# A recommendation tower whose table gathers are given places in the order of work, two by two

## What is computed

```python
e = jnp.stack([tbl_0[ids[:, 0]], ..., tbl_39[ids[:, 39]]], axis=1)        # 2048 x 40 x 32
z = jnp.einsum('bke,kef,bkf->bk', e[:, I], W, e[:, J])                     # 780 pairs i < j
h = jnp.concatenate([z, dense_ctx], axis=1)                                # 2048 x 796
h = jnp.maximum(h @ W_top1 + b_top1, 0.0)                                  # 512
h = jnp.maximum(h @ W_top2 + b_top2, 0.0)                                  # 256
y = h @ W_top3                                                             # 1
```

## Time and profile before

| | us |
|---|---|
| timed, median of 3 | 632.92 |
| profiled execution, span of its core | 1130.1 |
| TensorE (matmul) busy in it | 875.4 |
| VectorE busy | 540.3 |
| POOL busy | 412.3 |
| ScalarE busy | 327.1 |

### The profile page before, as it was taken

How to read it: one execution, slowest core, us unless ns; L and a number is a source line. 1 busy time by engine, 2 the same in 40 slices (tenths; PEclk the granted TensorE clock), 3 DMA queues, 4 the chain that set the end, 5 groups by cost and what they waited for, 6 DMA issues and landing times.

```text
span 1130.1 us, 16792 instructions
## 1 busy us (share of the span) xinstructions
PE 875.4 (77%) x7232; PEld 201.8 (18%) x7232; DVE 540.3 (48%) x510; ACT 327.1 (29%) x243; POOL 412.3 (36%) x436
## 2 busy tenths in 40 slices
PE   4322358788779995886895789779889787899998
PEld 1000012121112220121121112112112111122223
DVE  3100067364345660452380447337245264688884
ACT  4001047553246380032260134127244000000002
POOL 6777341533353137324517151451624604000000
PEclk8555598887578895886796788989779788899999
DMA  4100044201001020100101002010010102011010
GB/s 155 32 14 13 12 145 127 63 7 52 9 11 53 12 72 13 44 16 18 38 22 41 5 10 75 9 47 4 12 34 8 39 3 58 8 39 29 1 36 3
DMA packets 30489, 39.24 MB, mean 35 GB/s; under 512 B 11376, under 2 KB 19200, under 8 KB 30160
## 3 DMA queue, kind: packets, MB, share of 16 engines
q1 hardware_dynamic: 14880, 25.59, 7.7%
q0 software_dynamic: 13824, 7.11, 4.3%
q10 hardware_dynamic: 1712, 5.48, 1.4%
HBM read 21.93 MB, written 0.07 MB: 19 GB/s over the span
## 4 chain that ended last, share of the span: by engine, by line
PE 65%; another core or an unknown queue 17%; issue 11%; DVE 3%; ACT 2%; SPq 1%; DMA 1%; DVEq 0%; ACTq 0%
PE t_ps L857 27%; PE z_ps L881 18%; PE x_ps L898 10%; PE x_ps L806 7%; PE x_ps L911 2%; SPq L543 1%; DVE prod L727 1%; ACT one_hot L602 1%; PE t_ps L911 1%; DVE one_hot L689 1%; PE t_ps L898 1%; PE t_ps L829 0%; DVE z_sb L673 0%; ACT one_hot L605 0%
## 5 line engine op out<-in xcount | busy, mean ns | idle before, releaser
L727 DVE TENSOR_TENSOR prod<-t_ps,e_t 128x1024 f32<-128x1024 f32 x392 | 459.4, 1213 | 425.2 <-remote 300.6
L558 POOL DMA_INDIRECT rows<-cold_tables,idx x432 | 412.1, 954 | 550.1 <-DVE e_t L734 420.2
L857 PE MATMUL t_ps<-e_t,w_sb 32*64 32x512 f32 x3120 | 362.0, 658 | 73.8 <-issue 53.6
L881 PE MATMUL z_ps<-prod,select 128*32 128x512 f32 x1560 | 243.5, 639 | 21.7 <-issue 21.0
L602 ACT ACTIVATE one_hot<-hot_sb,row_number 128x2048 bf16<-128x2048 f16 (+1 forms) x75 | 140.6, 1875 | 110.3 <-remote 87.4
L898 PE MATMUL x_ps<-z_sb,w_sb 128*32 128x512 f32 x704 | 131.1, 635 | 24.4 <-issue 22.5
L605 ACT ACTIVATE one_hot<-one_hot 128x2048 bf16<-128x2048 bf16 (+1 forms) x75 | 134.3, 1791 | 2.4
L857 PEld LDWEIGHTS t_ps<-e_t,w_sb 32*64 32x64 f32 x3120 | 74.6, 136 | 323.0 <-issue 221.6
L806 PE MATMUL x_ps<-one_hot,tables 128*32 128x512 bf16 x1194 | 97.8, 402 | 27.3 <-issue 22.6
L806 PE MATMUL t_ps<-one_hot,tables 128*32 128x512 bf16 x198 | 45.3, 501 | 92.1 <-issue 87.9
L689 DVE TENSOR_SCALAR one_hot<-hot_sb,row_number 128x2048 bf16<-128x2048 f16 (+1 forms) x47 | 33.9, 744 | 133.2 <-remote 130.0
(11 more groups left out here) (33 smaller groups left out, 98.6 us busy)
## 6 DMA issues: line engine op xcount, KB each, us to landing
e_t<-e_t SPq DMA_DIRECT2D x64, 128.0 KB
e_t<-e_t SPq DMA_DIRECT2D x112, 64.0 KB
rows<-cold_tables,idx POOLq DMA_INDIRECT x432
hot_sb<-hot_ids SPq DMA_DIRECT2D x11, 512.0 KB, 3.6
w_sb<-w_lay ACTq DMA_DIRECT2D x1, 1792.0 KB, 7.0
z_sb<-hot_tables SPq DMA_DIRECT2D x4, 320.0 KB, 5.1
w_sb<-w_lay ACTq DMA_DIRECT2D x1, 1216.0 KB
w_sb<-w_lay ACTq DMA_DIRECT2D x1, 896.0 KB, 4.6
```

The costliest lines, as they stand in the source:

```text
L558: pool.indirect_dma_start(out=rows[:, slot, span, :], out_offset=None, in_=table, in_offset=bass.IndirectOffsetOnAxis(ap=idx[:, n, span:sp ...
L727: nc.vector.tensor_tensor(prod[:, u % PROD_SLOTS, 0:banks, :], t_ps[:, at:at + banks, :], by, ALU.mult).then_inc(mult_done, 1)
L857: mm = nc.tensor.matmul(t_ps[cols, at + n, :], w_sb[part, b, cols], e_t[part, e_slot(k, of[side]), :], start=True, stop=True)
L881: mm = nc.tensor.matmul(z_ps[E * q:E * q + E, :], select[:, E - PER - PER * s:2 * E - PER - PER * s], prod[:, (u + q // 2) % PROD_SLOTS, q ...
```

## The change

`ORDER` is replaced by another string of 837 letters with the same steps, three of whose one-hots are VectorE's instead of ScalarE's (50 `o`, 72 `O`). A list `PACE` gives each item a first place and, by the next entry, an end. The 16 gathers of an item are issued in twos (`TOGETHER = 2`), each two at a place of its own, spread evenly between the item's first place and its end. Before each two POOL waits until the last generating burst ahead of that place has been multiplied by VectorE, or the last lookup ahead of it has been done, whichever of the two kinds stands last in the order. The wait for the slot stays. The core of the diff:

```diff
 ORDER = """
-pippppipphpoohoOppoohopphpohOppohpoophphpopohhhooOhpoohpohhopohphhpotopOhhohhhpgpoophhhphOhrhoohhoooppghhhOooh
...
+pppppippopooppOppihohpohhphhoopoopoppOopphhoohoOhOpppohohhopphhhohohhOoohphhpgohpohOhprhohhpohohpoophhhooOhoOg
...
+PACE = [
+    0, 59, 89, 119, 149, 179, 209, 251, 275, 299, 330, 354, 382, 406, 445, 469, 493, 517, 541, 565,
+    589, 613, 637, 661, 685, 709, 733, 763,
+]
+TOGETHER = 2
+
+
+def pace_of(n, span):
+
+    begin, end = PACE[n], PACE[n + 1]
+    return begin + (end - begin) * (span - span % TOGETHER) // SPANS
...
+        def wait_for_pace(engine, place):
+
+            for kind, *of in reversed(steps[:place]):
+                if kind == "gen":
+                    engine.wait_ge(mult_done, first_unit(*of) + 2)
+                    return
+                if kind == "hot" and of[2] < blocks[of[1]] - 1:
+                    engine.wait_ge(looked_up, looked_up_to[tuple(of)])
+                    return
...
                 for span in range(SPANS):
+                    if span % TOGETHER == 0:
+                        wait_for_pace(pool, pace_of(n, span))
                     pool.indirect_dma_start(
```

More of the change, by code:

```diff
@@ L164 @@
 ORDER = """
-pippppipphpoohoOppoohopphpohOppohpoophphpopohhhooOhpoohpohhopohphhpotopOhhohhhpgpoophhhphOhrhoohhoooppghhhOooh
[L166 to L172, removed]
+pppppippopooppOppihohpohhphhoopoopoppOopphhoohoOhOpppohohhopphhhohohhOoohphhpgohpohOhprhohhpohohpoophhhooOhoOg
+hhghhotOrOgOrhgrghhgrgOrtrgrhghOhgrgOhorgrOrghOgtrOhgrrgrOghOrgrgOhOOhgrtrghrghOhgrhOogrrghhgrgOrrtgOhrghhgrgt
+rOrOOghrgOhhgorrgrhOghrgOhhgrOorghrghhgOrgorhgrrOghOrgOhrghrghrtg11g1rg1OrOg11grrtgO1rg1rtOg11g1rgr1grrghrgrOh
+grhgorhgrOhhgrOohgohrgthhrgo11g1O1trOgO11grOrrghhgrrohOgrhogrhOhghOhgrhgtrrgrhg1rg1rgOtO1rg1rg11grrg2rg2rg2rg2
+rgO2rg2Org22ghrgrhOghrghrghhgrOrogrOthgrhg1rgo11grrgO1rOgO11grrg1rtgt11gr11gr1gOrrgohhOghrhgOOrhtgrrgOhrgrhgOr
+hhghrgrO1g11tgrO1ogr11gr33grrtOgOhrghrohghohrOghrohghrhgrhgr1g11gr1g11grr2gr2grrgr2tgt2rg22g2rgrgr2g3rgrrg3rg1
+rg1grg1rg1gr1gr1grtrg11gr1tgrrgr1g11grrgr1g1rgr1gt11gr1grrg11g1rtg1rgrg1rgr1grrg22gtr2g2rgrrgr2g22grrg2rg11gr1
+gr1tgr1grrg11grrg1rgr1g11gr1gr1g1rg1rgr1gr3gr3g1r1r1111112222222233
 """
```

## The result

| | before | after | ratio (95%) |
|---|---|---|---|
| timed, median (us) | 633.02 (632.90 to 633.54) | 640.89 (638.05 to 643.37) | 1.0113 (1.0077 to 1.0148) |

The change costs 7.9 us. The forecast was 631.0, with a range up to 638.5: wrong in sign, and outside its range.

What follows compares the result with a forecast made beforehand. TensorE's 594 us plus what the engines can't overlap was taken as bound: 612.0, 614.4 with copy and store, the gather stream at 620.3 perhaps binding the first half. Forecast: 632.9 - 1.9 = 631.0, range 624.5 to 638.5.

Steps and rivals of the forecast that it cites:

- what the places cost: POOL's waits before each two gathers: 0 us where the stream is behind, 6 us of holding back from item 14.
- (4): Places hold gathers back too long from item 14, VectorE stands at late turns: 3 to 7 us, 638; chance 0.11.
- my last sentence on what would show me wrong: Prediction also wrong if the clock's half-speed stretches are part of the timed run and the order moves them; no size.
- The jam: Profile's 1130.1 us against 632.92 timed: the 497 us between, while gathers run, taken as made by the recording.
- rival (5): The profile's jam costs the timed run too and spaced pairs relieve it: at most 18 us, half is 623; chance 0.10.
- forecast (1): Engines' fit before step 416 decides, more TensorE work in the first 50 bursts: -1.9 us, 631.0; chance 0.37.
- rival (3): Stream decides, met first at turn 5, where VectorE stands up to 7.2 us: +1.7 us, 634.6; chance 0.25.
- rival (2): Stream decides in both orders, met at step 416 with the same work behind: no change, 632.9; chance 0.17.
- 267.6 for item 12: Landing of item 12 in us, seven items of 20.0 us after item 5 at 127.4; turned at step 416.
- The three more one-hots of VectorE: One-hots moved from ScalarE hold up POOL's gathers: 3 x 0.44 = 1.3 us of the stream, or 7.4 by the page's figures.
- VectorE's 529: VectorE's work summed over the order's letters from single-instruction durations: 529 us.
- TensorE's 594: TensorE's work summed over the order's letters at full clock: 594 us.

Runs made afterwards that it cites:

- run 511: Not a run label: in "costs the timed run 511 us", 511 us is the jam's cost to the kernel before on one chip, 1144 less 633.
- turn5_later: New order without places, the turn of item 5 moved from step 219 to 238: 629.73 us beside 633.82 for the kernel before, 0.9932.
- places_earlier: Changed kernel with all places from item 6 on earlier, nearly all by 24 steps: 634.94 us beside 634.03, on a repeat 634.57 beside 633.82.
- after_turns_later: Changed kernel with all its places, turns of items 5 and 18 moved to steps 238 and 600: 630.81 us beside 633.83, 0.9950.

## Why the prediction was wrong

**The failed step: what the places cost.** I took 0 us where the stream is behind and 6 us of holding back from item 14, put turn 18 at 621.2 "0.9 over the old 620.3", and gave the loss (4) a chance of 0.11. The mechanism was right to the item: the sixth turn and one of the last ten stood, as listed, and (4)'s 638 is near the 640.9. The term that was mis-sized is the landing of item 18: 393.8 in my sum, 402.7 measured. Of the 8.9 us, 4.4 are the stream's own: without places item 18 lands at 392.2 and not at 387.8 (393.8 less the 6), for gathers beside VectorE's one-hots and table splits take up to 1.5 us instead of 0.95 (the starts of item 0's sixteen span 20.5 us and not 18.75; beside multiplications and turns alone none takes over 0.96), and item 12 begins at 250.3, not at 244.7 (4.7 + 12 x 20.0). The other 4.5 are the places, which hold back in three stretches and not in one: measured against the new order without them, item 13 begins 2.9 us later (273.2 against 270.3), where I had 0, item 14 7.7 (297.9 against 290.2), where I had 6 (my own 292 less 285 is 7), and item 18 lands 10.5 later. A place comes when the kernel comes to it, so the kernel's own lateness is in it: I had it at step 445 at 292, and POOL's wait there ended at 297.9. Turn 18 then comes at 403.0 with the 227.4 us of TensorE of my own sum behind it; with the turn's 0.7, the half clock's 1.7 and the end's 2.4 this gives 635.2, for a span of 636.3; the median execution has 2.8 us more, by its clock. The half level after a wait was in no term at all, only in my last sentence on what would show me wrong. And I compared two bounds from zero, 621.2 and 620.3, neither of which is the moment that counts. What decides is where VectorE stands when item 18 lands (398.6 against 402.7), and that I never worked out. My excuse against (4), 12 us from an item's last place to its turn, looked at the last pair alone and not at how late the stream comes to it.

**The jam.** "I take it as made by the recording" was wrong as said: on one chip it costs the timed run 511 us (1144 less 633), and rival (5), for which I allowed at most 18 us, is there the whole result, 0.7587. For the chips of the result the reading gave the right kernel, 633 us without a jam, but by luck: a trace 1.8 times as long as the timed runs shows two conditions, and doesn't say which of them the next timed run meets. The expected "span well under 1130" came true, 636.3, but the twos did not do it: the kernel before has 631.3 there.

**The fit, forecast (1).** I expected -1.9 us from it, ahead of step 416 and nothing behind. Without the wait at turn 5 the order gives -4.1 (629.73), or -2.5 between the two profiles, all of it ahead of step 416; with the wait -0.4. So the place of the gain was right and its size too small, and the sum left out turn 5, which I had put into rival (3) as if the two excluded each other. They add, and the places come on top: from the kernel before -4.1, +3.7 for the turn, +7.5 for the places. (These are differences of one row of kernels, so that they sum up proves nothing. What tests the parts is that moving the two turns alone brings the changed kernel to 630.81.)

**Turn 5, rival (3).** "Up to 7.2 us" of VectorE; it stood 3.75 and cost 3.7, clock included. The mechanism was right, at half its bound. "Against: every start-up wait makes it less" was right as well.

**The stream as bound, rival (2) and the basis of (3).** Wrong for the kernel before: item 5 has 12.7 us of slack and item 12 2.5; half the gathers change nothing. 267.6 for item 12 was 4.8 us too early (272.4), and the engines were 12.9 us later than their bound of 262. The better the order, the nearer this bound is: in `turn5_later` turns 8 and 12 stand 0.9 and 0.7 us.

**The three more one-hots of VectorE.** They were to cost the stream 1.3 us, or 7.4 by the other figure that stands there. Neither is seen: item 12 begins at 250.3 in the new order without places and at 250.7 in the old.

**What held.** 1.25 us a gather in steady state, unchanged on every chip; a met wait costs POOL 0 (no longer gap where it was tried); VectorE's 529 (537.9) and, 3% short, TensorE's 594 (610.6 busy).

## What to carry to other kernels

When a free-running stream is given places, compare at each consumer two moments on the real clock, its data's arrival and its own turn; a hold anywhere upstream is carried to the consumer with the least slack, here 110 us later. Pacing and the order of its consumers are one design: the same places cost 11.5 us, 7.5 us or about 1 us, by where the turns stand, and one wrong turn hides all that the order gains. And if a trace and its timed runs differ by a factor, get the trace of the condition that was timed before summing anything, and expect the change to meet both.

## What the runs showed of the chip

One and the same kernel, the one before, takes 633 us on three chips and 1144 on a fourth at the time of these runs, with the same gathers 1.25 us apart in both. Where it takes 1144, TensorE issues 7 matmuls from 60 to 80 us instead of 252 (the new order without places), at half clock, at beats of 0.70 us and with the DMA engines 9% busy. Stopping POOL between twos until VectorE has got on brings it to 867.

A wait of VectorE that lets TensorE run dry can cost more than it lasts. A gap of 3.1 us on TensorE was followed by some 3.4 us at half clock in the changed kernel; a gap of 2.2 us by some 6.8 us of it in one profile of `places_earlier` and by none in another of the same program, where the gap was 2.1; a gap of 1.5 us at turn 8 of `after_turns_later` by some 3.4 us; and the gap of 2.3 us at turn 5 of the changed kernel by none.

A gather of 0.95 us takes up to 1.5 beside one-hots and table splits of VectorE in the new order without places, and no longer than 0.96 beside its multiplications from PSUM or its turns.
